# Perceiver layer on one core: norm, weight split and part of V of self-attention moved into cross-attention, x loaded by quads

## What is computed

```python
q = split_heads(layernorm(x) @ Wq); k, v = split_heads(ctx @ Wk), split_heads(ctx @ Wv)   # 16 heads of 16
x = x + (softmax(q @ k.T) @ v) @ Wo                      # cross-attention, 256 keys
q, k, v = layernorm(x) times wq, wk, wv                  # 16 heads of 64
x = x + causal_softmax(q @ k.T / 8) @ v @ wo.T           # self-attention, 64 keys
h = gelu(quantized(layernorm(x)) @ quantized(W_in) + b_in)
x = x + quantized(h) @ quantized(W_out) + b_out          # feed-forward, width 1024
```

## Time and profile before

| | us |
|---|---|
| median of 3 runs | 637.76 |
| lowest and highest | 636.15, 639.42 |
| the profiled execution, as timed | 638.59 |
| its span, first to last instruction | 636.8 |
| PE busy in the span | 591.1 |
| DVE, ACT, POOL busy | 464.2, 377.1, 190.2 |
| mean granted TensorE clock | 0.983 |

### The profile page before, as it was taken

One profiled execution on the slowest core, in us unless ns is written; L12 is line 12 of the kernel. 1 busy time (PEld: TensorE's weight loads), 2 busy tenths in 40 slices (PEclk: granted clock), 3 DMA queues, 4 the chain that ended last, 5 costly groups with the idle time before them and its releaser, 6 DMA issues. The chain is left out here.

```text
span 636.8 us, 17469 instructions
## 1 busy us (share of the span) xinstructions
PE 591.1 (93%) x6765; PEld 514.9 (81%) x6770; DVE 464.2 (73%) x977; ACT 377.1 (59%) x1011; POOL 190.2 (30%) x243
## 2 busy tenths in 40 slices
PE   6689999999999899997798999999999999899897
PEld 3578888898889788996687888888989898644597
DVE  4557788888878778875899756565666656678797
ACT  3567788888878788873322424343433333558884
POOL 6522233333333333672411212121212111260400
PEclk9789999999999999999899999999999999999999
DMA  6995767777768768840400000000000000000012
GB/s 205 259 245 147 196 150 192 161 204 158 209 149 205 162 166 220 209 154 1 134 2 11 3 3 1 3 1 2 3 3 1 2 3 2 2 0 2 0 50 83
DMA packets 37073, 58.93 MB, mean 93 GB/s; under 512 B 6913, under 2 KB 15233, under 8 KB 36993
## 3 DMA queue, kind: packets, MB, share of 16 engines
q1 hardware_dynamic: 29328, 42.75, 26.7%
q10 hardware_dynamic: 4592, 8.78, 4.9%
q0 software_dynamic: 3072, 6.30, 4.2%
HBM read 17.96 MB, written 2.10 MB: 31 GB/s over the span
## 5 line engine op out<-in xcount | busy, mean ns | idle before, releaser
L704 ACT ACTIVATE Pr<-pS,nmax 128x256 f32<-128x256 f32 x256 | 120.0, 483 | 27.0 <-DVE nmax L818 25.9
L818 DVE TENSOR_REDUCE nmax<-pS 128x2 f32<-128x512 f32 x128 | 87.4, 683 | 23.5 <-PE pS L542 22.2
L1045 POOL TENSOR_TENSOR a_Pr<-a_Pr,a_rinv 128x512 f32<-128x512 f32 x32 | 32.7, 1044 | 182.9 <-DVE a_rinv L1327 182.9
L552 PE MATMUL pT<-ident,Pr 128*128 128x128 f32 x512 | 78.9, 277 | 2.7 <-DVE wraw L823 2.4
L542 PE MATMUL pS<-Kst,Qst 96*128 96x256 f32 x256 | 59.1, 314 | 14.4 <-ACT Pr L704 5.5
L1213 ACT ACTIVATE a_Pr<-a_Pr 128x512 f32<-128x512 f32 x32 | 20.2, 631 | 78.9 <-DVE a_Pr L1319 78.9
L552 PEld LDWEIGHTS pT<-ident,Pr 128*128 128x128 f32 x512 | 60.4, 143 | 3.9 <-issue 3.9
L542 PEld LDWEIGHTS pS<-Kst,Qst 96*128 96x128 f32 x256 | 40.8, 196 | 22.7 <-issue 12.1
L704 ACT ACTIVATION_READ_ACCUMULATOR Pr<-pS,nmax 128x1 f32 x256 | 54.8, 214 | 0.0
L324 POOL DMA_DIRECT2D Qst<-QSh x60 | 30.3, 508 | 75.1 <-PE pS L542 71.4
L59 PE MATMUL a_pJ<-Kst,XTh 128*128 128x512 f32 x64 | 27.9, 437 | 3.0 <-ACT a_V L1208 3.0
(11 more groups left out here) (365 smaller groups left out, 2079.6 us busy)
## 6 DMA issues: line engine op xcount, KB each, us to landing
Kst<-WO_ints SPq DMA_DIRECT2D x96, 128.0 KB, 3.3
CT<-ctxT ACTq DMA_DIRECT2D x16, 512.0 KB, 5.0
Kst<-KSh SPq DMA_DIRECT2D x62, 128.0 KB, 3.1
Qst<-QSh POOLq DMA_DIRECT2D x64, 64.0 KB, 3.1
Qst<-QSh SPq DMA_DIRECT2D x64, 64.0 KB, 2.8
Kst<-KSl SPq DMA_DIRECT2D x31, 128.0 KB, 3.3
Qst<-QSl POOLq DMA_DIRECT2D x32, 64.0 KB, 2.8
Qst<-QSl SPq DMA_DIRECT2D x32, 64.0 KB, 2.7
```

The source lines that it names most:

```text
L552: last = pe.transpose(pT[s % 2][:, t, k, :], Pr[s % 2][:, t, P * k:P * k + P], ident[:, :])
L704: act.activation(Pr[c % 2][:, t, :], pS[c % 2][:, t, :], ACT.Exp, bias=nmax[c % 2][:, t:t + 1], accum_out=rsum[par][:, c // 4, 2 * (c % 4) ...
L818: dve.tensor_reduce(nmax[s % 2][:, :], pS[s % 2][:, :, :], AX.X, ALU.max, negate=True).then_inc(maxed, 1)
L1045: pool.tensor_tensor(rows, rows, rinv[s][:, :].unsqueeze(2).to_broadcast([P, 8, SQ]), ALU.mult).then_inc(weighted, 1)
```

## The change

1. SP loads x in eight loads of one quad (256 KB). Quads 2 and 3 are issued behind the second pair's K, quads 4 to 7 at the head of bodies 0 to 3. DVE waits for `x_in[i + 2]` at step 4 of every quad up to the sixth.
2. The second pair's K is restacked in two parts: group 0 (three DMAs) ahead of that pair's Q, groups 1 to 3 (nine) behind it.
3. ACT issues the context load of pair 3 at step 2 of the first quad and no longer ahead of the first exponential.
4. The norm of self-attention's quad 1 is made in cross-attention's last quad: statistics at step 4 and `normalize` at step 12 on DVE, `rstd` on POOL between `split_high(1)` and `split_low(1)`.
5. POOL makes the low part of the output weights behind the high part, in cross-attention, when all scores are done; it lies in `Qst1`.
6. Parts 0 and 1 of V of self-attention's first quad are made in cross-attention (events `SV`), between `turn_o`, `turn_back` and `project_out` of the last pair; ACT copies one half of each bank and DVE the other. Self-attention's first quad has two events less, and the counts of its waits are changed to match.

```diff
-            load_x(0, 2, x_in0)
+            load_x(0)
             for m in W_ORDER[1:]:
                 load_w(m)
-            load_x(2, 2, x_rest[0])
+            load_x(1)
...
             restack_first_q(sp, qst_sync[0], (0, 1))
+            restack_k(sp, 1, 7, 0, (0,))
             restack_q(sp, qst_sync[1], 1, 3, 0, (0, 1))
-            load_x(4, 4, x_rest[1])
-            restack_k(sp, 1, 7, 0)
-            load_x(8, 8, x_rest[2])
+            restack_k(sp, 1, 7, 0, (1, 2, 3))
+            load_x(2)
+            load_x(3)
...
                 if not last:
+                    if i + 4 < QUADS:
+                        load_x(i + 4)
                     restack_k(sp, 0, EV0 + EV * i + 2, CHUNKS * (2 * i + 1))
...
             split_high(1)
+            rstd_of(QUADS + 1)
             pool.wait_ge(proj, BEFORE_LAST + 3)
             split_low(1)
...
-            pool.tensor_copy(shared.WO_high, raw[:, 3, :])
+            pool.tensor_copy(shared.WO[HI], raw[:, 3, :]).then_inc(weights_high, 1)
+            pool.wait_ge(weights_high, 3 * KC + 1)
+            pool.wait_ge(scores, CHUNKS * PAIRS)
+            pool.tensor_tensor(shared.WO[LO], raw[:, 3, :], f32(shared.WO[HI]), ALU.subtract)
...
+                elif kind == "SV":
+                    pe.wait_ge(weights_split, 3)
+                    last = split_matmul(pe, bank[:, :], parts(XT, slice(0, P)),
+                                        shared.weights(2, slice(512 * part, 512 * part + 512)))
...
-            load_ctx(3, 1, 2)
             exps(0, 0)
...
+                    if s == 2 and first:
+                        load_ctx(3, 1, 2)
...
-                    if s == 4 and first:
-                        dve.wait_ge(x_rest[1], 16)
-                    if s == 12 and first:
-                        dve.wait_ge(x_rest[2], 16)
-                    if s == 4 and i + 2 <= QUADS:
+                    if s == 4 and two_ahead(i):
+                        dve.wait_ge(x_in[i + 2], 16)
+                    if s == 4:
                         statistics(i, i + 2)
...
-                    if s == 8 and i + 2 <= QUADS:
+                    if s == (12 if last else 8):
                         normalize(i + 2)
...
-            statistics(1)
-            normalize(1)
-
```

## The result

| | before | changed |
|---|---|---|
| median | 636.75 us (20 runs) | 640.04 us (20 runs) |
| lowest and highest | 633.87, 639.42 | 637.17, 643.46 |
| the profiled execution, as timed | 638.59 | 637.71 |
| its span | 636.8 | 636.0 |

The changed kernel takes 1.0054 of the time before (95% interval 1.004 to 1.0069), 3.4 us more. So I read single stretches in them, not their sum, and took more traces of both kernels.

The account below looks back on a forecast made before the run. PE was taken to bound the kernel, with gains possible only at the start and the seam between the attentions. Seam -2.9 and start +1.9 gave -1.0 us: 636.8 on a median of 637.76, range 633.2 to 640.6.

Parts of the forecast that it names:

- the start: First quad: PE goes on with step 8 at 44.9 instead of 42.98 us, held through DVE's wait for x; 1.9 us lost.
- the seam: Between cross- and self-attention: -5.0 for the earlier first `shift`, +1.5 for half clock, +0.6 for the norm; -2.9 us.
- the case that had a chance of 0.16: Rival, last quad: the norm's second half falls behind POOL's 4.56 us subtraction; 4.4 us over forecast, 641.2; chance 0.16.
- The landing of x: Start: quad 2's x, issued at 36.0 us, lands at 42.3 by counted bytes; earliest 41.4, latest 43.6.
- I price the half clock behind it as before: Start: PE's idle time before step 8 grows from 3.0 to 4.9 us, with no new cost for 1.2 GHz behind it.
- the 5.0 of the sum: Seam: DVE can make self-attention's first `shift` at 304.1 instead of 309.09, so PE gets to `X` 5.0 us earlier.
- the 1.5 that I gave back: Seam: `X` transposes, turns and Q part run at 1.2 GHz behind PE's wait; 1.5 us lost, bounds 0 and 2.5.
- The norm's cost in the good case: Cross-attention's last quad: the norm at step 12, held by POOL's copy, makes the last `weigh` 0.6 us later.

Follow-up runs that it names:

- ctx_old: The changed kernel with the second-next context load back at its old place, ahead of the first exponentials: 637.51 us, 1.0032 of before.
- seam_only: The kernel before with points 4 to 6 of the change alone and the old start: 635.64 us, 0.9986 of before.
- low_self: The changed kernel with POOL's low part of WO back at the head of self-attention: 636.25 us, 0.9990 of before.
- best: The changed kernel with SP's old start order (x by quads), norm behind `scale_o`, POOL's low part of WO at self-attention's head: 628.76 us, 0.9907 of before.
- after_again: The changed kernel itself, run once more for a second trace: 640.28 us, 1.0066 of before.
- x2_first: The changed kernel with x of quad 2 loaded ahead of the first part of the second pair's K on SP: 634.74 us, 0.9985 of before.

## Why the prediction was wrong

Two terms of the sum failed: the start, taken as +1.9 us, cost 3.8, and the seam, taken as -2.9, gave 0.5 on average, because the case that had a chance of 0.16 came in four of six traces.

1. **The landing of x, mis-sized.** The mechanism was right to the name: DVE held at step 4, PE at step 8 by ACT's exponential, and no other wait. I took the landing at 42.3 and PE at 44.9; x landed at 43.9, PE went on at 46.80. The upper bound of 43.6 was too low as well. (The working has a slip of its own: 10.0 us from 32 on end at 42.0.) The load took 7.6 us from an issue at 36.3 where the sum has 6.3 from 36.0, so it landed 1.6 us late, and from DVE's statistics to PE's score it was 2.9 us, not 2.6: together the 1.9. The rate and the context loads were right (247 GB/s measured, and 4.0 us for two context loads in `ctx_old`); the bytes were 0.47 MB too few, 1.9 us at that rate. Those that I left out of the sum are the x loads of quads 3 and 4, issued right behind; that it is they is argued from the bytes, and the cause of the 1.6 us stays open as far as experiments go.
2. **The reference of the start.** "I price the half clock behind it as before" rests on one execution of before, in which PE stood and fell to 1.2 GHz. In the second it did neither and reached the last score 2.9 us earlier. Of the 3.8 us at step 8 the two first traces keep 2.9 at the last score; against the mean of the old starts it is 3.8 again, by chance. So the start's term should have read 3.8 where it read 1.9; this is the same 1.9 as in point 1, not one more.
3. **The seam's good case, right in its sum by errors that cancel.** From the last score to the end of the span the two traces without the collision have 3.7 and 2.3 us less than before; I had -2.9. The terms were others. DVE's first row maximum of self-attention came 10.79 us after the last `weigh` (308.60 - 297.81) instead of 14.34 before, 3.6 less and not the 5.0 of the sum: 1.7 us went to the barrier, where POOL holds everybody for 8.19 us after its last instruction, a term that the sum doesn't have. And the 1.5 that I gave back for a halved clock behind the `X` event came only in part: in the first trace eight turns took 1.04 us, as at full clock, and it is 320.3 us to the end; in `seam_only` the same eight took 1.89 and it is 321.5. With the barrier mended (`low_self`, `best`) the distance to `X` is 21.5, 5.5 us less than before, so the -5.0 was a fair price of the mechanism itself.
4. **The rival that I gave 0.16 came in four of six traces.** Place and order of the instructions were as written. In `after_again` the last row maximum stands 6.34 us behind the last score instead of 0.52, so 5.8 late (I had 6.5), the last `weigh` 10.45 instead of 5.58, so 4.9 late (about 5), and the executions with it took 3.3 us more (4.4). What failed is the step from "it decides from a shift of 0.1 us between two free-running lists" to a chance. I kept the one order that the two numbers of one trace gave (289.0 before 289.1), where such a margin is a coin's toss or worse. I also compared its 641.2 us as a case of its own, where it is a mixture inside every measurement. Half the chance on it would have moved the forecast of the seam from -2.9 to -0.7.
5. **The norm's cost in the good case.** The last `weigh` came 5.74 us after the last score against 5.58: 0.16, not 0.6 (in `seam_only`, with a pair of 2.74 us, 0.5).

Together: the start 1.9 worse than forecast, the seam 2.4 worse as a mixture (-0.5 for -2.9), which leads from -1.0 to +3.3, against 3.4 measured.

## What to carry to other kernels

Where an SBUF-to-SBUF instruction of DVE and a long one of POOL come within a few tenths of a microsecond of each other on lists that nothing ties together, take both orders as real, price the worse one, and move one of them to where the other engine is idle (here 3.4 us for moving two instructions). Of a load moved in a queue, ask who waits for it first and what bytes go ahead of it on every queue, and of an edge between stages ask what each engine's last instruction is: here POOL's last one had to end 8.2 us ahead of the first matmul behind the barrier to be free. Look at more than one execution before a term of 2 us is taken from it.

## What the runs showed of the hardware

- From the end of POOL's last instruction in cross-attention to the first matmul of self-attention it is 8.19 or 8.20 us in seven traces where POOL ended late, with a subtraction of 4.6 us and with a memset of 0.10 us as its last.
- The outcome of this meeting of DVE and POOL is not spread but in two groups: in the six traces of the changed kernel 2.3 to 2.4 us or 6.3 to 6.8 us for the same two instructions, with nothing between.
- A wait of PE in the middle of its work can cost more than a later start. With the first score at 25.69 us PE stood 3.01 us at step 8 and ran at 1.2 GHz behind it; with the first score at 29.08, in another execution of the same program, it did not stand, kept 2.4 GHz and was 2.9 us earlier at the end of cross-attention. In `x2_first` it stood 1.66 us there and kept 2.4 GHz.
- The granted clock behind a wait differs between executions of one program. In the 8 us from the first `X` event on it was 1.00, 0.79 or 0.63 in the traces of the changed kernel, and the rest of the span 320.3, 321.5 or 322.2 us.
- A load's time to land hangs on what else is in the queues: 256 KB of x, issued at 36.0 to 36.3 us behind the same twelve K restacks, landed after 7.6 us with two context loads of 512 KB issued in the 5 us before it (the changed kernel) and after 3.9 us with none (`ctx_old`).
